# A graph kernel's gather loops: ten buffers for three, a skewed order of work, and 400 steps of 125-row gathers for 391 of 128 rows

## What is computed

```python
def gcn_conv(x, edge_index, edge_weight, W, b, n_nodes):   # twice, with relu between
    deg = segment_sum(ew, col, n_nodes)                    # ew: weights, self-loops 1
    dinv = where(deg > 0, rsqrt(deg), 0)
    norm = dinv[row] * ew * dinv[col]
    h = x @ W
    out = segment_sum(h[row] * norm[:, None], col, n_nodes)
    return out + b

def gin(x, edge_index, edge_attr, We, be, W1, b1, W2, b2, gamma, beta):
    msg = relu(x[src] + edge_attr @ We + be)               # edge_attr: 200000 x 32
    h = x + segment_sum(msg, dst, n_nodes)
    h = relu(h @ W1 + b1) @ W2 + b2
    return relu(batch_norm(h) * gamma + beta)

x = x + log_softmax(gcn(relu(layernorm(x)), ...))
x = x + gin(relu(layernorm(x)), ...)
```

## Time and profile before

| | us |
|---|---|
| median of 3 timed runs | 6395.15 |
| their lowest and highest | 6393.17, 6398.4 |
| span of the profiled execution | 7443.2 |

### The profile page before, as it was taken

How to read it: one execution, slowest core, us unless ns; L and a number is a source line. 1 busy time by engine, 2 the same in 40 slices (tenths; PEclk the granted TensorE clock), 3 DMA queues, 4 the chain that set the end, 5 groups by cost and what they waited for, 6 DMA issues and landing times.

```text
span 7443.2 us, 65119 instructions
## 1 busy us (share of the span) xinstructions
PE 3143.2 (42%) x13129; PEld 2504.6 (34%) x13130; DVE 1940.5 (26%) x6985; ACT 882.4 (12%) x3744; POOL 4606.9 (62%) x4769
## 2 busy tenths in 40 slices
PE   5333333333333533333333333355555555555556
PEld 5322222222222522222222222243333334333334
DVE  3222222222222322222222222252222222222223
ACT  3100000000000200000000000031111111111113
POOL 3566666666666366666666666656666666666665
PEclk5555555555555555555555555556666555656656
DMA  1111111111111211111111111122222222221111
GB/s 41 50 34 33 34 34 33 34 34 33 34 34 33 55 34 34 33 34 34 33 34 34 34 33 34 34 62 45 47 46 46 45 46 46 46 45 44 44 44 48
DMA packets 227042, 293.10 MB, mean 39 GB/s; under 512 B 97266, under 2 KB 147464, under 8 KB 226889
## 3 DMA queue, kind: packets, MB, share of 16 engines
q0 software_dynamic: 150144, 230.70, 14.8%
q1 hardware_dynamic: 76870, 62.08, 2.9%
HBM read 273.19 MB, written 19.25 MB: 39 GB/s over the span
## 4 chain that ended last, share of the span: by engine, by line
POOL 32%; issue 28%; another core or an unknown queue 14%; PE 11%; DVE 6%; DMA 4%; ACT 3%; DVEq 2%; POOLq 0%; ACTq 0%; SPq 0%
POOL rows_g L404 32%; PE psum L747 8%; DMA rows_g<-table,idx 4%; DVE hot L1044 3%; PE psum L694 1%; ACT rows_g L542 1%; DVEq L261 1%; PE psum L781 1%; ACT idx L523 1%; DVE rows_g L1061 1%; DVE acc L1052 1%; ACT attr L522 0%; PE psum L725 0%; PE psum L864 0%
## 5 line engine op out<-in xcount | busy, mean ns | idle before, releaser
L404 POOL DMA_INDIRECT rows_g<-table,idx x4692 | 4444.1, 947 | 2603.7 <-issue 1331.2
L747 PE MATMUL psum<-hot,rows_g 128*96 128x128 f32 x9384 | 2208.9, 415 | 3997.2 <-DMA rows_g<-table,idx 2231.7
L747 PEld LDWEIGHTS psum<-hot,rows_g 128*96 128x96 f32 x9384 | 1895.5, 266 | 4376.5 <-issue 3038.6
L1052 DVE TENSOR_TENSOR acc<-acc,psum 96x128 f32 x1173 | 332.2, 283 | 4591.9 <-PE psum L747 2411.2
L522 ACT ACTIVATE attr<-edge 128x12 f32 (+1 forms) x1173 | 248.8, 212 | 5844.4 <-PE psum L747 3503.9
L1041 DVE TENSOR_SCALAR hot<-iota,attr 128x128 f32<-128x128 f32 x3128 | 828.6, 355 | 277.5 <-issue 247.5
L736 PE MATMUL psum<-we_blk,eaT 128*128 128x384 f32 (+1 forms) x782 | 533.9, 854 | 140.7 <-ACT eaT L538 95.2
L736 PEld LDWEIGHTS psum<-we_blk,eaT 128*128 128x128 f32 (+1 forms) x782 | 241.1, 329 | 349.7 <-issue 349.7
L1044 DVE TENSOR_SCALAR hot<-iota,attr 128x128 f32<-128x128 f32 x1564 | 324.4, 302 | 103.1 <-issue 103.1
L1061 DVE TENSOR_TENSOR rows_g<-rows_g,psum 128x384 f32<-128x384 f32 x391 | 213.8, 547 | 277.0 <-DMA rows_g<-table,idx 233.6
L542 ACT ACTIVATE rows_g<-rows_g 128x384 f32<-128x384 f32 x391 | 200.6, 513 | 391.4 <-DVE rows_g L1061 317.7
(11 more groups left out here) (136 smaller groups left out, 840.2 us busy)
## 6 DMA issues: line engine op xcount, KB each, us to landing
rows_g<-table,idx POOLq DMA_INDIRECT x4692
ea<-in_edge_attr_dram SPq DMA_DIRECT2D x390, 64.0 KB
table<-tab SPq DMA_DIRECT2D x13, 840.0 KB
tab<-in_x_dram SPq DMA_DIRECT2D x100, 46.9 KB
x_sb<-in_x_dram SPq DMA_DIRECT2D x1, 4200.0 KB
out_dram<-x_sb SPq DMA_DIRECT2D x5, 840.0 KB
x_more<-in_x_dram SPq DMA_DIRECT2D x3, 840.0 KB
table<-tab SPq DMA_DIRECT2D x13, 97.5 KB
```

The source lines that it names most:

```text
L404: pool.indirect_dma_start(out=rows_g[u][0:np_, g * F:(g + 1) * F], out_offset=None, in_=table[p], in_offset=bass.IndirectOffsetOnAxis(ap=i ...
L747: last = pe.matmul(ps_agg[u], rows_g[u][0:np_, g * F:(g + 1) * F], hot[u][0:np_, g, :], start=g == 0, stop=g == G - 1)
L1052: dve.tensor_tensor(a, a, ps_agg[u], ALU.add).then_inc(fast.added, 1)
```

## The change

- A step has 500 edges in four groups of EP = 125. That makes exactly 400 equal steps, and the short one is gone (TP = 0). Every gather has 125 rows, and every load of edge features 125 partitions.
- `idx`, `attr` and `rows_g` have U = 10 slots, `hot` and `ea` have H = 5, the PSUM banks of the aggregation, the edge term and the transposes two each. Some buffers lie in memory that is free at that time (`x_more`, `rows_g`) to make room.
- The order is skewed: a turn has ten steps, and in it each step's parts stand alone. VectorE builds the hot matrices three steps ahead (LA = 3) and then adds the window of the present step. In the third pass TensorE transposes three steps ahead (LT) and multiplies by `We` two steps ahead (LL), ScalarE copies one transpose per step, and stages the slot of the step before.
- The last ten steps are written out behind the loop. Ten warm-up matmuls (`warm`) stand before the last step of each pass; before, they stood before the short step of the first two passes.
- The degree batches have DK = 2 sets of buffers and 20 turns of two batches instead of 13 turns of three and a short one.
- The log-softmax work comes in 25 turns of four columns (JX, XI) instead of 100 turns of one.

```diff
+    EP = 125
     G = 4
-    GE = G * P
+    GE = G * EP
-    U = 3
+    U = 10
+    H = 5
+    LA = 3
+    LT, LL = 3, 2
     ITERS = FULL // U
     DG = 10
-    DK = 3
+    DK = 2
...
-        rows_g = [sb(f"rows_g{u}", [P, G * F]) for u in range(U)]
-        hot = [sb(f"hot{u}", [P, G, W]) for u in range(U)]
-        ea = [sb(f"ea{u}", [P, G * KE]) for u in range(U)]
-        eaT = sb("eaT", [P, U * P])
+        rows_t = sb("rows_g", [P, U * G * F])
+        rows_g = [rows_t[:, u * G * F:(u + 1) * G * F] for u in range(U)]
+        hot_t = sb("hot", [P, (H - 1) * G * W])
...
-        ps_agg = [bank[u][0:F, 0:W] for u in range(U)]
-        ps_e = [bank[3 + u][:, 0:G * F] for u in range(U)]
+        ps_agg = [bank[k][0:F, 0:W] for k in range(2)]
+        ps_e = [bank[3 + k][:, 0:G * F] for k in range(2)]
...
-                each_group(pool, lambda s, it, u, np_: gather(fast, p, s, u, np_, fast_got[u]))
+                with pool.Fori(0, ITERS - 1) as it:
+                    for k in range(U):
+                        t = Step(it, k)
+                        gather(fast, p, t.s, t.u, EP, fast_got[t.u])
+                for t in last_steps():
+                    gather(fast, p, t.s, t.u, t.np_, fast_got[t.u])
...
+            def gin_iter(it):
+                for k in range(U):
+                    t = Step(it, k)
+                    gin_copy(Step(it, k + LL))
+                    relu_msg(fast, t.s, t.u, EP)
+                    if k >= 1:
+                        stage_fast(2, Step(it, k - 1 + U))
+                stage_fast(2, Step(it, 2 * U - 1))
...
+            def aggregate_pass(p):
+                with pe.Fori(0, ITERS - 1) as it:
+                    for k in range(U):
+                        aggregate(p, Step(it, k))
+                for t in last_steps():
+                    if t.s == NS - 1:
+                        warm(WARM)
+                    aggregate(p, t)
+                pe.wait_ge(fast.added, fast.banks + (p + 1) * NS)
...
+            with pe.Fori(0, ITERS - 1) as it:
+                for k in range(U):
+                    gin_transpose(Step(it, k + LT))
+                    gin_linear(Step(it, k + LL))
+                    aggregate(2, Step(it, k))
...
-            def build_hot(p, s, u, np_):
-                dve.wait_ge(fast.staged, p * NS + s + 1)
+            def build_hot(p, t):
+                n = p * NS + t.s
+                np_ = t.np_
+                dve.wait_ge(fast.staged, n + 1)
+                dve.wait_ge(fast.agg, n + 1 + U - H)
...
+                def full(it):
+                    w = windows(dve, mybir.EngineType.DVE, it * U, U, win_row)
+                    for k in range(U):
+                        t = Step(it, k)
+                        build_hot(p, Step(it, k + LA))
                         if p == 2:
-                            add_edge_term(fast, s0 + u, it, u, np_)
-                            if u >= 1:
-                                add_window(p, s0 + u - 1, u - 1, w[u - 1])
+                            add_edge_term(fast, t.s, t.it, t.u, t.b, EP)
+                            if k >= 1:
+                                add_window(p, Step(it, k - 1), w[k - 1])
                         else:
-                            add_window(p, s0 + u, u, w[u])
+                            add_window(p, t, w[k])
```

## The result

The changed kernel takes 7803.1 us (7800.5 to 7804.7, four runs) where the kernel before takes 6394.3 on the same chip: 1.220 times as long, 95% interval 1.219 to 1.222. I had said 6537 and a range up to 7150.

What follows compares the result with a forecast made beforehand. GpSimd's gathers, one behind another at 1.252 us, were taken to bound the timed kernel. From 6385 us without stalls, +135 - 13 + 20 gave 6527, plus 10 to the median 6537 us; range 5950 to 7150.

Steps and rivals of the forecast that it cites:

- 125 rows for 128: Gathers of the three passes: 3 rows less on 4800 gathers, 0.9 ns per row, give -13 us.
- My own upper bound: GpSimd's gather time goes by the fullest engine's rows: 17 more at 14.7 ns, +1200 us in all, 7737 us.
- the cheap case: A 125-row gather in the passes costs about what the 80-row ones suggest, 0.94 us busy, -13 us in all.
- The stall: GpSimd's waits for ScalarE's index copy in the passes, 1058 us, belong to the traced execution, not the timed kernel.
- the rival's number: Stalls in the passes are real when timed, deeper rings remove 1058 us, a gather takes 1.029: 5458 us; chance 0.15.
- The test that I named, span against median: Changed kernel's span to median: some 10 us if stalls came from tracing, over 1000 us if they were real.
- Deeper rings, 0 us: Deeper slots and skewed order in the passes remove slot waits: 0 on the timed kernel, 1058 us as other bound.
- the 1.05 us gather: A gather beside VectorE work, used to size a moderately dearer 125-row gather: +0.11 us, 7065 us; dearer gather's chance 0.20.
- 108 more gathers, +135 us: 400 steps for 391 in three passes: 108 gathers more at 1.252 us, all on the path, +135 us.
- Degree stage, +20 us: Ahead of the first pass: seven more loop turns at up to 4.0 us, taken as +20 us, bounds 0 and 35.
- Five-engine transfer and edge loads, 0 us: Gathers' landing lengthens by half a microsecond, hidden by ten slots; edge loads change likewise with five buffers: 0 us.
- Last pass, no new wait: Third pass's chain stays under 5.0 us per step, costing nothing; rival of a new wait +80, 6620 us, chance 0.03.

## Why the prediction was wrong, point by point

- **125 rows for 128: the step that failed.** I took -13 us from the 80-row gathers, "being nearest in form". Measured +1285 us (6518.3 to 7803.1). The nearest in form was the wrong neighbour, since 80 rows also spread over sixteen engines. I had priced the number of rows, at 0.9 ns each. What costs is the rows on the fullest engine, 25 there for 8: a gather takes 1.219 us for 0.951. My own upper bound, 17 more rows on the fullest engine at 14.7 ns, gave +1200 and 7737 us; it was worked out from these rows and from the earlier trace rows, I left only 0.05 for all above 7150, and the measured time lies 66 us above even that bound. The SP load in the earlier trace rows showed five engines for 125 rows, and nothing but that one row stood for the cheap case. The Trainium skill, DMA: Bandwidth & Descriptors, section "Why a DMA increments its semaphore by 16 and not by 1", says that a DMA takes the largest number of engines up to 16 that divides its slowest dimension. The runs agree for these gathers (15 packets with rows, 25 rows on each of five engines), and the exception for direct copies doesn't show in them.
- **The stall.** That the timed kernel runs gather behind gather was right for the chips on which the times were taken, and gathers are no shorter there: 1.25 us from start to start (5881.9 us for 4692), not 1.029. The reason I gave, tracing, was wrong; it is the chip, and it was luck that the kernel was timed on a quick one, where that 0 holds. On the chips where the stall is real the rival's number fails as well: the deeper rings give 40 us, not 1058. I had the rings right for rows and indices and left out of the account that the banks of the aggregation go from three to two, for which TensorE waits there. The test that I named, span against median, couldn't tell, because both came from one chip this time. I also read the earlier trace rows wrong where I wrote that TensorE's matmuls of the following steps start in time. Those of 2368.92 don't: they wait for `hot` matrices, which VectorE builds only behind the add at 2366.41 that the late news held back:

```profile
2366.41 0.28 DVE L1052 TENSOR_TENSOR acc<-acc,psum 96x128 f32 x1 [8.80 <-remote]
...
2367.67 3.16 DVE L1041 TENSOR_SCALAR hot<-iota,attr 128x128 f32<-128x128 f32 x12 [0.97 <-issue]
```

- **Deeper rings, 0 us.** Measured +31 (6391.2 to 6421.9): GpSimd's gathers are busy 30 us longer, by the overlaps those beside the builds. I had a row for it, the 1.05 us gather in the earlier trace rows, and used it for another term.
- **108 more gathers, +135 us.** 6421.9 to 6518.3 is +96. In the traces (+93) the passes grow by 117 (5911 to 6028 us), 135 for the gathers less 19 for a shorter mean gather (0.951 us for 0.955), and the rest shrinks by 24, most of it the degree stage. The term was right.
- **Degree stage, +20 us.** Measured about -20 (first gather at 227.1 us for 245.9 on a quick chip). I counted turns and took 4.0 us for each; but these were the loads, 2.36 and 7.08 us by turns, and they are dear by where they begin more than by their number.
- **Five-engine transfer and edge loads, 0 us.** Right: landing went from 2.5 to 3.1 us, and GpSimd's idle time before a gather stayed 0.30. **Last pass, no new wait:** right, 2448 us for 2434, and GpSimd has no gap there.

From 6391 us the parts are +31, +96 and +1285, together 7803. That they add up is no check, since each is the difference of two measured times.

## What to carry to other kernels

Give an indirect gather a row count that spreads over all sixteen engines, and pad rather than trim: GpSimd pays for the fullest engine. Where a profile and the times of the same kernel differ, time and trace it on one more chip before you explain the difference or build against it. When rings are made deeper, list every buffer that a step waits for: the one that got shallower may take the gain. When a change makes something odd in size, bound it by the mechanism that the packets show, not by the row that looks most alike.

## What the runs showed of the hardware that I hadn't expected

- A gather of 127 rows keeps GpSimd busy 2.54 us, one of 125 rows 1.19, one of 128 rows 0.945; the packets per gather are 208, 64 and 32.
- A load of 20 to 30 numbers into TensorE's registers takes 1.36 to 2.36 us where it begins on a multiple of 16 bytes, and 6.15 to 7.08 us (26 and 30 numbers) 8 bytes behind one.
- Of five chips two took 7446 us for a kernel that takes 6391 to 6402 on the others, run after run, with the end of TensorE's work heard 3.1 us late in the mean, up to 10, and with deeper rings and two banks 9 us in the mean, up to 40.
- Gathers that start beside one of VectorE's selection builds keep GpSimd busy up to 0.1 us longer (1.06 for 0.95).
